# A nearer wait ahead of GpSimd's row fetches in layer 0 and layer 2 of a graph network

## The chip, the cores and the metric

The kernel runs on one core of one Trainium2 chip. The metric is the device time of one execution in microseconds. TensorE is called PE, GpSimd POOL and SyncE SP, as in the profile.

## The reference

Four graph layers run over one graph of 6250 nodes with 128 features and 100000 edges, sorted by destination. Each layer normalises the node features, gathers a row per edge at the edge's source, sums over the edges of each destination, and adds the result to the features. Cut to the sums that the changed code computes:

```python
# layer 0 (graph convolution with edge features)
agg  = segment_sum((nfeat * norm_src)[src], dst)
esum = segment_sum(efeat @ We + be, dst)
# layer 2 (relational, twice): one message table per relation
h    = einsum('ni,rio->rno', x, W)
msg  = h[etype, src]
mean = segment_sum(msg, dst * 8 + etype) / max(count, 1)
x    = mean.sum over relations + x @ W_root + b
```

Layers 1 and 3 are attention layers over the same edges.

## The kernel before, in words

The edges are cut into tiles of 128; there are T = 832 tiles, of which MOST = 829 have rows to fetch, and 52 steps of 16 tiles. Every layer is a pass over the tiles, written out in full (no loop on the chip). In each pass POOL fetches the 128 source rows of a tile from a table in HBM with one indirect DMA into a ring of R slots, VectorE makes a selection matrix from the tile's destinations, PE multiplies the selection by the rows, and VectorE adds the product to an accumulator of the node window that the tile belongs to. Between the tiles of a step PE, ScalarE and VectorE finish one node window: normalise, transpose, project, store.

The three functions of the change are `gather_first` (layer 0, "l0e", ring of R = 16, rows of 512 bytes beside the edge features that SP loads into the other half of each slot, L1028), `gather_relations` (first pass of layer 2, "l2e", R = 16, rows of 1 KB) and `gather_nodes` (second pass of layer 2, "l2f", R = 32, rows of 512 bytes). POOL does nothing in these passes but fetch. Its lines are L999, L2648 and L854. Before every fourth fetch, from tile R on, POOL waits for the semaphore `summed`, which PE raises once per multiplied tile (L1156 and L1157, L2766, L888); in the kernel before the value is `t - R + G`, the last use of the four slots that are written next:

```python
if t >= R and t % G == 0:
    pool.wait_ge(summed, t - R + G)
```

On PE's side, l0e and l2e wait for the rows of each tile by itself; l2f waits at every fourth tile for all four.

What else runs between the tiles of a step: in l0e PE transposes and multiplies the finished sums (L1164, L1165, L1170, L1171), transposes the normalised rows (L1176) and projects them (L1182). In l2e PE multiplies the finished window by the root (L2744) and by the eight relations (L2751, in two halves, at the third and the sixth tile of a step), and SP stores the message block (L2656) and loads the next step's destinations to all partitions (L2661), 512 KB each. In l2f PE transposes (L805) and projects (L818), at the ninth and thirteenth tile.

Of the kernel before, what the change touches and what calls it, by code (L numbers as in the profile page):

```python
# [67 lines left out]
def windows_of(nc, g, engine, first, count=4, at=TA, top=NW - 1):  # L68

    _, values = nc.values_load_multi_w_load_instructions(  # L70
        g.rows[0:1, bass.ds(first + at, count)], engines=(engine,), min_val=0, max_val=top,
        skip_runtime_bounds_check_because="tile_tables clamps every entry to this range")
    return values
# [758 lines left out]
def gather_nodes(nc, g, sem, name, table, index, coef, weights, biases, scale, queries):  # L832

    R = 32
    G = 4
    B = 6
    V = 4
    with Stage(nc, name) as st:
        rows = st.sb("rows", [P, R, D])  # L840
        sel = st.sb("sel", [P, V, G, P])
        ps = [st.ps(f"ps{b}") for b in range(B)]
        nodes = Nodes(nc, g, sem, st, name, weights, biases, False, scale, queries)
        gathered = [sem(f"{name}_g{r}") for r in range(R // G)]
        sel_made, summed, added = sem(name + "_sel"), sem(name + "_summed"), sem(name + "_added")

        with nc.Block() as block:
            @block.gpsimd
            def _(pool):
                for t in range(MOST):  # L850
                    n = t // G
                    if t >= R and t % G == 0:
                        pool.wait_ge(summed, t - R + G)
                    pool.indirect_dma_start(rows[:, t % R, :], None, table, bass.IndirectOffsetOnAxis(index[:, t:t + 1], 0)) \  # L854
                        .then_inc(gathered[n % (R // G)], 16)

            @block.sync
            def _(sp):
                nodes.load(sp)
                for k in range(NW):  # L860
                    if k % nodes.EACH == nodes.EACH - 1:
                        nodes.keep(sp, k)
                    if k >= 1:
                        nodes.store(sp, k - 1)
                nodes.store(sp, NW - 1)
                nodes.land(sp)

            @block.scalar
            def _(act):
                act.wait_ge(nodes.ready, 1)  # L870
                for k in range(NW):
                    act.wait_ge(added, min(S * (k + 3) + 12, T))
                    nodes.stats(act, k)
                    nodes.norm(act, k)
                    nodes.move(act, k)

            @block.tensor
            def _(pe):
                pe.wait_ge(nodes.ready, 1)
                for t in range(T):  # L880
                    n, i, r = t // G, t // S, t % S
                    if t % G == 0:
                        pe.wait_ge(sel_made, n + 1)
                        if t < MOST:
                            pe.wait_ge(gathered[n % (R // G)], 16 * (G * (n // (R // G)) + min(G, MOST - t)))
                    if t % 2 == 0 and t >= B:
                        pe.wait_ge(added, t - B + 2)
                    nc.tensor.matmul(ps[t % B][:, 0:D], sel[:, n % V, t % G, :], rows[:, t % R, :],  # L888
                                     start=True, stop=True).then_inc(summed, 1)
                    if i >= 4 and r == 8:  # L890
                        nodes.turn(pe, i - 4)
                    if i >= 4 and r == 12:
                        nodes.project(pe, i - 4, first=i == 4)
                for k in range(NS - 4, NW):
                    nodes.turn(pe, k)
                    nodes.project(pe, k)

            @block.vector
            def _(dve):
                windows = []  # L900

                def make_sel(n):
                    if n >= V:
                        dve.wait_ge(summed, G * (n - V + 1))
                    for s in range(G):
                        t = n * G + s
                        ins = nc.vector.tensor_scalar(sel[:, n % V, s, :], g.iota[:, :], g.dloc[:, t:t + 1],
                                                      coef[:, t:t + 1], ALU.is_equal, ALU.mult)
                    ins.then_inc(sel_made, 1)

                def add(t):
                    if t % S == 0:
                        windows[:] = windows_of(nc, g, mybir.EngineType.DVE, t, S)
                    x = nodes.x_of(windows[t % S])
                    if t % 2 == 0:
                        dve.wait_ge(summed, t + 2)
                    if t >= 1:
                        dve.wait_ge(added, t)
                    nc.vector.tensor_tensor(x, x, ps[t % B][:, 0:D], ALU.add).then_inc(added, 1)  # L919

                nodes.prepare(dve)
                make_sel(0)
                make_sel(1)
                for n in range(T // G):
                    i, q = n // (S // G), n % (S // G)
                    if n + 2 < T // G:
                        make_sel(n + 2)
                    for s in range(G):
                        add(n * G + s)
                    if q == 1 and i >= 4:  # L930
                        nodes.scales(dve, i - 4)
                    if q == 2 and i >= 4:
                        nodes.join(dve, i - 4)
                    if q == 3 and i >= 4:
                        nodes.add_bias(dve, i - 4, first=i == 4)
                for k in range(NS - 4, NW):
                    nodes.scales(dve, k)
                    nodes.join(dve, k)
                    nodes.add_bias(dve, k)

def gather_first(nc, g, sem, a, queries, own):

    R = 16
    G = 4
    B = 4
    H = 8
# [5 lines left out]
    with Stage(nc, "l0e") as st:  # L954
# [38 lines left out]
        with nc.Block() as block:  # L993
            @block.gpsimd
            def _(pool):
                for t in range(MOST):
                    if t >= R and t % G == 0:
                        pool.wait_ge(summed, t - R + G)
                    pool.indirect_dma_start(rows[:, t % R, 0:D], None, table,  # L999
                                            bass.IndirectOffsetOnAxis(g.src_i[:, t:t + 1], 0)).then_inc(gathered[t % R], 16)  # L1000

# [1604 lines left out]
def gather_relations(nc, g, sem, name, table, index, width, acc, a):  # L2606

    R = 16
    G = 4  # L2610
    B = 5
    LAG = 3
    K3 = 3 * RELS
    with Stage(nc, name) as st:
# [19 lines left out]
        dv, split, selt_made, counted, marked, weighed, coef_made, sel_made, summed, added = (  # L2634
            sem(f"{name}_{k}") for k in ("dv", "split", "selt", "counted", "marked", "weighed", "coef", "sel", "summed",
                                         "added"))
# [5 lines left out]
        with nc.Block() as block:  # L2642
            @block.gpsimd
            def _(pool):
                for t in range(MOST):
                    if t >= R and t % G == 0:
                        pool.wait_ge(summed, t - R + G)
                    pool.indirect_dma_start(rows[:, t % R, :], None, table,  # L2648
                                            bass.IndirectOffsetOnAxis(index[:, t:t + 1], 0)).then_inc(gathered[t % R], 16)

# [234 lines left out]
def layer2(nc, g, sem, a):  # L2885

    with Stage(nc, "l2") as st:
        acc = st.sb("acc", [P, NW * HID])

        gather_relations(nc, g, sem, "l2e", g.msg1_d.rearrange("n (r f) -> (n r) f", r=RELS), g.msg_i, HID, acc, a)

def layer3(nc, g, sem, a, out):

    H = 2
    AW = D + H
    with Stage(nc, "l3") as st:
        acc = st.sb("acc", [P, NW * AW])
        with Stage(nc, "l3t") as tables:  # L2900
            queries = tables.sb("queries", [P, NP])
            gather_nodes(nc, g, sem, "l2f", g.msg2_d.rearrange("n (r f) -> (n r) f", r=RELS), g.msg_i, g.coef,
                         [a["L3_gnn_Wv"], a["L3_gnn_Wk"], a["L3_gnn_Wq"]],
                         [a["L3_gnn_bv"], a["L3_gnn_bk"], a["L3_gnn_bq"]], 64.0 ** -0.5, queries)
            sem.give_back()
            attention_edges(nc, g, sem, "l3te", H, queries, False, acc, AW,
                            lambda st: Outputs(nc, g, sem, st, a, out, acc))
# [92 lines left out]
```

## Time and profile before

| | us |
|---|---|
| median of 3 runs | 6026.54 |
| lowest, highest run | 6025.05, 6029.79 |
| span of the profiled execution | 7205.4 |
| POOL busy in it | 4079.2 (57%) |
| PE busy in it | 4349.8 (60%) |
| VectorE busy in it | 3857.3 (54%) |

The profiled execution is known by its span alone; no other time of it is given. It is longer than every timed run by about 1179 us. Busy times count an engine's instructions without its waits. A PE time is modelled at its end. "Issue" is time in which an engine waited for nothing that the profile shows. A fetch's time on POOL is that of its issue; its landing is not among the rows. A wait that is put down to a DMA of another stage, or to "remote", is one whose releaser the profile could not tell.

### The profile page before, as it was taken

What the parts mean: (1) busy time and instruction counts of PE and PEld (TensorE: products, weight loads), DVE (VectorE), ACT (ScalarE), POOL (GpSimd) and SP (SyncE); (2) the same over time, 40 slices, a digit from 0 to 9 for tenths busy, and PEclk for the clock granted to TensorE, in tenths of its full rate; (3) what the DMA queues carried; (4) which work ended last, traced back from release to release, by engine and by line L of the source; (5) the groups of instructions that cost most, each with busy time, mean ns of one, the idle gap of its engine ahead of it and who ended that gap; (6) DMA issues with size and microseconds to landing.
All of it is one profiled execution on the core that took longest, in us unless ns stands there. A gap on an engine that the chain in (4) does not pass through costs nothing. (4 is left out here: it accounts for less than half of the span.)

```text
span 7205.4 us, 86034 instructions
## 1 busy us (share of the span) xinstructions
PE 4349.8 (60%) x19030; PEld 3531.2 (49%) x19030; DVE 3857.3 (54%) x11927; ACT 1461.9 (20%) x3928; POOL 4079.2 (57%) x4191
## 2 busy tenths in 40 slices
PE   4777778746566656795666666344343456665656
PEld 4666666635555555444444444233333345555555
DVE  7444444446566656745555555344444455666655
ACT  4122222212222222350111111000000112222222
POOL 1666666646566554106666665666666555555553
PEclk9977776766666666897888888555555566667676
DMA  2433333323333334274444444122222333333333
GB/s 49 126 108 102 100 101 100 100 87 109 106 108 107 105 99 84 82 286 125 135 129 136 128 136 109 51 60 56 59 56 59 74 100 113 106 110 113 108 112 64
DMA packets 426775, 738.44 MB, mean 102 GB/s; under 512 B 100523, under 2 KB 280580, under 8 KB 419701
## 3 DMA queue, kind: packets, MB, share of 16 engines
q0 software_dynamic: 173200, 436.47, 23.0%
q1 hardware_dynamic: 244484, 289.62, 12.2%
q10 hardware_dynamic: 8592, 6.82, 0.3%
q8 instruction: 176, 2.88, 0.2%
q14 instruction: 323, 2.64, 0.1%
HBM read 613.55 MB, written 120.20 MB: 102 GB/s over the span
## 5 line engine op out<-in xcount | busy, mean ns | idle before, releaser
L1637 POOL DMA_INDIRECT xh<-pair_d,src_i x1658 | 1647.5, 994 | 1191.6 <-issue 459.2
L2648 POOL DMA_INDIRECT l2e_rows<-msg_d,msg_i x829 | 804.8, 971 | 749.3 <-POOLq L61 315.4
L999 POOL DMA_INDIRECT l0e_rows<-node_d,src_i x829 | 789.0, 952 | 450.4 <-issue 220.4
L854 POOL DMA_INDIRECT l2f_rows<-msg_d,msg_i x829 | 782.7, 944 | 431.4 <-issue 231.9
L1156 PE MATMUL l0e_ps<-l0e_rows,l0e_sel 128*128 128x256 f32 x1664 | 795.2, 575 | 282.3 <-issue 232.8
L888 PE MATMUL l2f_ps<-l2f_rows,l2f_sel 128*128 128x128 f32 x1664 | 413.1, 417 | 600.1 <-DVE xh L919 501.0
L2766 PE MATMUL l2e_ps<-l2e_rows,l2e_sel 128*128 128x256 f32 x1664 | 490.0, 427 | 422.5 <-DVE l2e_sel L2860 396.4
L888 PEld LDWEIGHTS l2f_ps<-l2f_rows,l2f_sel 128*128 128x128 f32 x1664 | 367.3, 310 | 674.7 <-issue 394.9
L2825 DVE TENSOR_TENSOR l_acc<-l_acc,l2e_ps 128x256 f32 x832 | 349.4, 420 | 498.4 <-DMA node_d<-l1t_queries 329.0
L919 DVE TENSOR_TENSOR xh<-xh,l2f_ps 128x128 f32 x832 | 238.3, 286 | 675.5 <-DMA tb_raw<-edges_d,starti 470.7
L1221 DVE TENSOR_TENSOR early_acc<-early_acc,l0e_ps 128x264 f32 x832 | 356.8, 429 | 441.0 <-PE l0e_ps L1157 168.6
L2766 PEld LDWEIGHTS l2e_ps<-l2e_rows,l2e_sel 128*128 128x128 f32 x1664 | 328.6, 212 | 534.6 <-DVE l2e_sel L2860 424.8
L1681 PE MATMUL l1te_pq<-l1t_queries,l1te_wide 128*128 x1664 | 353.9, 380 | 327.8 <-DVE l1te_prod L1895 225.6
L1681 PE MATMUL l3te_pq<-l3t_queries,l3te_wide 128*128 x1664 | 350.1, 377 | 314.2 <-DVE l3te_prod L1895 216.2
L1156 PEld LDWEIGHTS l0e_ps<-l0e_rows,l0e_sel 128*128 128x128 f32 x1664 | 367.9, 271 | 326.9 <-issue 252.1
L1157 PEld LDWEIGHTS l0e_ps<-l0e_of_rel,l0e_sel 128*128 128x128 f32 x1664 | 452.2, 272 | 103.0
L2022 DVE TENSOR_TENSOR l1acc_acc<-l1acc_acc,l1te_ps 128x144 f32 x832 | 246.6, 296 | 466.9 <-DMA l0e_rows<-in_edge_attr_dram 259.9
L1681 PEld LDWEIGHTS l1te_pq<-l1t_queries,l1te_wide 128*128 128x128 f32 x1664 | 310.9, 279 | 372.6 <-issue 372.3
L2022 DVE TENSOR_TENSOR l_acc<-l_acc,l3te_ps 128x130 f32 x832 | 234.9, 282 | 475.7 <-remote 263.7
L1681 PEld LDWEIGHTS l3te_pq<-l3t_queries,l3te_wide 128*128 128x128 f32 x1664 | 306.7, 276 | 353.8 <-issue 352.5
L1733 PE MATMUL l1te_ps<-l1te_ve,l1te_sel 128*128 128x144 f32 x1664 | 398.4, 402 | 19.9 <-DVE l1te_ve L2006 18.2
L1733 PE MATMUL l3te_ps<-l3te_ve,l3te_sel 128*128 128x130 f32 x1664 | 361.0, 378 | 54.8 <-DVE l3te_ve L2006 18.1
(454 smaller groups left out, 8180.8 us busy)
## 6 DMA issues: line engine op xcount, KB each, us to landing
l0e_rows<-in_edge_attr_dram SPq DMA_DIRECT2D x832, 64.0 KB
msg_d<-l1t_queries SPq DMA_DIRECT2D x50, 1024.0 KB, 3.9
l1te_local<-local_d SPq DMA_DIRECT2D x52, 512.0 KB
l2e_local<-local_d SPq DMA_DIRECT2D x52, 512.0 KB
l3te_local<-local_d SPq DMA_DIRECT2D x52, 512.0 KB
xh<-pair_d,src_i POOLq DMA_INDIRECT x1658
msg_d<-l2e_msg SPq DMA_DIRECT2D x50, 512.0 KB
l0e_rows<-node_d,src_i POOLq DMA_INDIRECT x829
```

The source lines that it names most:

```text
L854: pool.indirect_dma_start(rows[:, t % R, :], None, table, bass.IndirectOffsetOnAxis(index[:, t:t + 1], 0)) \
L888: nc.tensor.matmul(ps[t % B][:, 0:D], sel[:, n % V, t % G, :], rows[:, t % R, :], start=True, stop=True).then_inc(summed, 1)
L999: pool.indirect_dma_start(rows[:, t % R, 0:D], None, table, bass.IndirectOffsetOnAxis(g.src_i[:, t:t + 1], 0)).then_inc(gathered[t % R], 16)
L1156: nc.tensor.matmul(ps[r % B][:, 0:2 * D], sel[:, r // G % 2, r % G, :], rows[:, r, :], start=True, stop=True)
L1157: nc.tensor.matmul(ps[r % B][:, 2 * D:W0], sel[:, r // G % 2, r % G, :], of_rel[:, r // G % 2, r % G, :], start=True, stop=True).then_inc( ...
L1221: nc.vector.tensor_tensor(one, one, ps[s][:, 0:W0], ALU.add).then_inc(added, 1)
L1637: pool.indirect_dma_start(rows[:, t % R, :], None, g.pair_d, bass.IndirectOffsetOnAxis(g.src_i[:, t:t + 1], 0)).then_inc(gathered[n % RG], 16)
L1681: mm = nc.tensor.matmul(pq[n % 2][:, i * D:(i + 1) * D], wide[:, n // GS % 2, n % GS * G + i, :], queries[:, bass.ds(ws[i] * D, D)], start ...
L1733: nc.tensor.matmul(slot(t), sel[:, n % V, t % G, :], ve[:, n % V, t % G, :], start=True, stop=True).then_inc(summed, 1)
L2022: nc.vector.tensor_tensor(part, part, slot(t), ALU.add).then_inc(added, 1)
L2648: pool.indirect_dma_start(rows[:, t % R, :], None, table, bass.IndirectOffsetOnAxis(index[:, t:t + 1], 0)).then_inc(gathered[t % R], 16)
L2766: nc.tensor.matmul(ps[t % B][:, 0:width], sel[:, t // G % 2, t % G, :], rows[:, t % R, :], start=True, stop=True).then_inc(summed, 1)
```

## The change

In the three functions a constant NEAR = 8 takes the place of R in the wait's condition and in its value. The slots, the order of the fetches and everything on the other engines stay. So ahead of the fetches of tiles t to t + 3 POOL waits until t - 4 tiles are multiplied, in place of t - 12 (l0e, l2e) or t - 28 (l2f).

```diff
@@ gather_nodes
     R = 32
+    NEAR = 8
...
-                    if t >= R and t % G == 0:
-                        pool.wait_ge(summed, t - R + G)
+                    if t >= NEAR and t % G == 0:
+                        pool.wait_ge(summed, t - NEAR + G)
@@ gather_first
     R = 16
+    NEAR = 8
...
-                    if t >= R and t % G == 0:
-                        pool.wait_ge(summed, t - R + G)
+                    if t >= NEAR and t % G == 0:
+                        pool.wait_ge(summed, t - NEAR + G)
@@ gather_relations
     R = 16
+    NEAR = 8
...
-                    if t >= R and t % G == 0:
-                        pool.wait_ge(summed, t - R + G)
+                    if t >= NEAR and t % G == 0:
+                        pool.wait_ge(summed, t - NEAR + G)
```

## Rows read from the trace of the kernel before

**Rows 1.** Head of the page.
```profile
span 7205.4 us, 86034 instructions
```

**Rows 2.** Stretches l0e, l2e, l2f: us, busy PE, PEld, DVE, ACT, POOL (instructions); clock, DMA.
```profile
207.00:1454.00 1247.00, 973.05 (x3760) 824.38 (x3760) 601.17 (x2037) 286.00 (x782) 788.98 (x829) 0.75 0.38 104
3235.00:4489.00 1254.00, 786.47 (x3516) 570.72 (x3517) 691.26 (x1974) 135.79 (x346) 804.79 (x829) 0.84 0.44 130
4507.00:5712.00 1205.00, 476.03 (x1808) 387.98 (x1808) 499.48 (x1903) 104.40 (x389) 782.70 (x829) 0.57 0.23 56
```

**Rows 3.** The page's groups, fetches: xcount | busy, mean ns | idle before, releaser.
```profile
L1637 POOL DMA_INDIRECT xh<-pair_d,src_i x1658 | 1647.5, 994 | 1191.6 <-issue 459.2
L2648 POOL DMA_INDIRECT l2e_rows<-msg_d,msg_i x829 | 804.8, 971 | 749.3 <-POOLq L61 315.4
L999 POOL DMA_INDIRECT l0e_rows<-node_d,src_i x829 | 789.0, 952 | 450.4 <-issue 220.4
L854 POOL DMA_INDIRECT l2f_rows<-msg_d,msg_i x829 | 782.7, 944 | 431.4 <-issue 231.9
```

**Rows 4.** l2f: a step in time order, a stretch's busy time; waits (total, times, longest).
```profile
5101.37 0.47 PE L805 MATMUL l2f_pt<-ident,l2f_pairs 128*128 128x128 f32 x1 [2.68 <-issue]
...
5103.35 1.49 PE L818 MATMUL l2f_po<-l2f_w,l2f_ht 128*128 128x384 f32 x2
...
5109.60:5116.40 6.80, 0.00 (x0) 0.00 (x0) 0.00 (x0) 0.00 (x0) 2.94 (x4) 0.52 0.15 39
...
5116.65 0.94 POOL L854 DMA_INDIRECT l2f_rows<-msg_d,msg_i  x1 [3.20 <-DMA tb_raw<-edges_d,starti]
...
5119.78 1.79 PE L888 MATMUL l2f_ps<-l2f_rows,l2f_sel 128*128 128x128 f32 x6 [1.19 <-DVE xh L919]
...
DVE xh L919 <- DMA tb_raw<-edges_d,starti: 470.7, 84, 10.5
```

**Rows 5.** Start of l2f in order of time: start, length, engine, line [idle before, releaser].
```profile
4511.34 0.95 POOL L854 DMA_INDIRECT l2f_rows<-msg_d,msg_i  x1 [0.30 <-issue]
...
4514.26 2.05 PE L888 MATMUL l2f_ps<-l2f_rows,l2f_sel 128*128 128x128 f32 x8 [11.91 <-DMA l2f_rows<-msg_d,msg_i]
...
4516.33 0.95 POOL L854 DMA_INDIRECT l2f_rows<-msg_d,msg_i  x1 [0.30 <-issue]
...
4517.59 0.94 POOL L854 DMA_INDIRECT l2f_rows<-msg_d,msg_i  x1 [0.30 <-issue]
...
4518.97 1.40 PE L888 MATMUL l2f_ps<-l2f_rows,l2f_sel 128*128 128x128 f32 x5 [2.66 <-DMA l2f_rows<-msg_d,msg_i]
```

**Rows 6.** Busy time by stretch, the six outside the five gathering passes: their sum.
```profile
sum 739.00, PE 492.95 PEld 306.39 DVE 440.53 ACT 302.54 POOL 55.84; mean PE 82.16 PEld 51.07 DVE 73.42 ACT 50.42 POOL 9.31
```

**Rows 7.** One step of l2e: in order of time, and busy time of one stretch.
```profile
3901.92 1.88 PE L2751 MATMUL l2e_pm<-l2e_w,l2e_ht 128*128 128x512 f32 x4
...
3904.77 1.32 POOL L2648 DMA_INDIRECT l2e_rows<-msg_d,msg_i  x1 [0.30 <-PE l2e_ps L2766]
...
3907.60 0.34 SPq L2656 DMA_DIRECT2D msg_d<-l2e_msg  x1
...
3908.00 0.42 SPq L2661 DMA_DIRECT2D l2e_local<-local_d  x1
...
3907.60:3912.60 5.00, 3.30 (x26) 2.27 (x24) 1.77 (x6) 0.34 (x2) 3.78 (x4) 1.00 0.71 246
```

**Rows 8.** One step of l0e: busy time of the step, and PE's other work in order.
```profile
899.70:923.60 23.90, 17.64 (x73) 15.15 (x72) 11.38 (x40) 5.97 (x18) 15.31 (x17) 0.71 0.36 101
...
902.57 0.77 PE L1170 MATMUL l0e_pz<-l0e_w,l0e_z 128*128 128x128 f32 x2
...
903.14 0.63 PE L1171 MATMUL l0e_pz<-l0e_w,l0e_z 128*128 128x128 f32 x2
...
903.56 0.42 PE L1176 MATMUL l0e_ph<-ident,l0e_hc 128*128 128x128 f32 x1
...
909.06 1.63 PE L1182 MATMUL l0e_pv<-l0e_w,l0e_ht 128*128 128x384 f32 x2
```

## The prediction

> **What bounds the kernel now.** I read the span first [rows 1], then the three passes that the diff touches, as stretches [rows 2]: 1247, 1254 and 1205 us, in which no engine is full. TensorE (PE) is busy for 78%, 63% and 40% of them, GpSimd (POOL) for 63 to 65%. In the profiled execution GpSimd is therefore not the bound of these passes: the fetch lines of the page [rows 3] show it idle for 450 us in layer 0 and 431 us in the second pass of layer 2 ahead of its fetches, of which 220 and 232 us are the fixed gap between two fetches ("issue") and the rest mostly waits on the products; in the first pass of layer 2 it is 749 us, 315 of them ahead of the pass. That is the ring at work: the fetches run as far ahead as it lets them.
>
> The profiled execution is not the execution that is timed. Its span is 7205.4 us [rows 1], 1179 us more than the median of 6026.5 us, and the reader should see where such time can sit. In the second pass of layer 2 ("l2f") there is a stretch of 6.8 us in which PE, VectorE and ScalarE do nothing, and GpSimd issues four fetches and stops [rows 4]; VectorE's waits of this kind in l2f are 84, 470.7 us in all, for 52 steps of 16 tiles. Whether the timed runs have the holes no row shows. What the rows do show is a floor: a fetch takes 0.952, 0.971, 0.944 and 0.994 us in layer 0, the first and the second pass of layer 2, and the attention passes [rows 3], and each follows the one before at 0.30 us [rows 5]. So 829 x 1.252 + 829 x 1.271 + 829 x 1.244 + 1658 x 1.294 = 1038 + 1054 + 1031 + 2145 = 5268 us of GpSimd in the five gathering passes. What lies outside them takes 739 us [rows 6]. Together 6007 us, 0.3% under the median. My estimate is that in the timed runs the holes are mostly gone and GpSimd's cadence is close to being the bound of all five passes, which makes any microsecond that GpSimd waits a microsecond of the result.
>
> **What the change does.** It removes and adds no work: no fetch, no product, no DMA. The wait rides on the first of four fetches; ten more of some 600 such fetches get one (two more in each ring of 16, six in the ring of 32), at no cost of their own. It moves the moment: the fetch of tiles t to t+3 needs all products through tile t-5. GpSimd can be four to eight tiles ahead of PE, and no longer up to 16 or 32. Behind the waiting fetch on GpSimd stand only later fetches; who waits for them is PE, and behind PE VectorE's additions. SP's transfers wait on other counts and are not held.
>
> **The loop that is new, and its slack.** From the end of the issue of tile t-5 to GpSimd's turn for tile t pass four fetches and five gaps, 4 x 0.95 + 5 x 0.30 = 5.3 us. In that time tile t-5 must land and be multiplied, or GpSimd stops. For the landing I take the start of l2f, where PE waits for nothing but the fetched rows [rows 5]: the fourth fetch ends at 4512.29 and PE starts at 4514.26, the eighth ends at 4517.28 and PE starts at 4518.97. So landing and signal take at most 1.7 us. This bound serves for all three passes.
>
> l2f: PE takes four tiles at once. The same rows give the slack directly: the first four products end at 4516.31, and GpSimd's turn for the ninth tile is at 4517.59: 1.28 us to spare, with GpSimd never stopped. What eats it, once a step, is PE's other work between the tiles: the projection, 1.49 us, and a transpose, 0.47 us, in neighbouring groups [rows 4]. The projection alone overruns by 1.49 - 1.28 = 0.21 us, both together by 0.68. From 11 to 35 us over 52 steps; nothing in the rows says how much they add up, so I take the middle, 24 us.
>
> First pass of layer 2 ("l2e"): PE's busy time is 786.5 / 832 = 0.95 us a tile, other work included [rows 2]. A tile is asked for 4 x 0.971 + 5 x 0.30 = 5.38 us after its issue, so the slack is 5.38 - 1.7 - 0.95 = 2.7 us. PE's message products between two tiles, 1.88 us, fit [rows 7]. What may not fit is SP's pair of transfers of 512 KB each (sizes from the code), issued 0.4 us apart; the stretch behind them moves 246 GB/s at 71% of the DMA engines' time [rows 7]. 1 MB at that rate is 4.3 us, so a fetch that shares the engines with it lands between 0 and 4.3 us later. Over the slack that is 0 to 1.6 us a step, 0 to 83 us; I take half, 42 us, since the engines are neither free nor full there. Today this is hidden by the rows already fetched.
>
> Layer 0 ("l0e"): a step of 16 tiles has 17.64 us of PE [rows 8], 1.1 us a tile; slack 5.3 - 1.7 - 1.1 = 2.5 us. PE's other work comes in pieces of 0.77 + 0.63 + 0.42 = 1.82 us and 1.63 us [rows 8]. Each fits; if PE has not caught up between them, they overrun by 3.45 - 2.5 = 0.95 us, 49 us in all. PE's 17.64 us against 16 x 1.252 = 20.0 us of GpSimd say that it mostly does catch up, so I take a third, 16 us.
>
> Once per pass GpSimd also stops after eight fetches while the stage is set up; that is a fetch or two, and I leave it in the range. Sum: 24 + 42 + 16 = **82 us**. Against the profiled execution that would be 7205 + 82; against the median, 6026.5 + 82 = **6108 us**, 1.4% slower. All bounds low give 11 us more, all high 35 + 83 + 49 = 167.
>
> **Rivals.** First, GpSimd is the bound and the wait never ends last: then fetched rows do not pile up at all, and the place of the wait is of no matter. This is the start of l2f prolonged over all passes [rows 5]. It holds as long as PE's delay behind a landing stays under 1.28 us in l2f, 2.7 in l2e and 2.5 in l0e, and the first that passes these decides against it. Time: **6026 us**. For it speaks the floor of 6007; against it the 1.49 us projection and SP's 1 MB.
>
> Second, the holes are in the timed runs too. Then PE works in bursts behind each, and the fetched pile feeds the burst. In l2f GpSimd's own wait ends at 5116.65, at the end of the hole [rows 4]; the fourth fetch from there ends 3 x 1.244 + 0.94 = 4.67 us later, and lands by 5123.0. PE wants that group at the third tile of its six records, at 5119.78 + 2/3 x 1.79 = 5121.0. Late by 2.0 us, 104 us over 52 steps; with l2e and l0e at their upper bounds, 104 + 83 + 49 = 236 us: **6262 us**. For it speaks every step of the profile; against it that the median is 1179 us shorter than that profile.
>
> Third, a small gain: fetches now issue at other moments beside VectorE. One fetch of l2e took 1.32 us where 0.94 is usual [rows 7]. If one such a step moves out of its way, 0.38 x 52 = 20 us: **6006 us**. But nothing says that the new moments are quieter.
>
> **The numbers.** Forecast 6108 with 0.48; second rival 0.23; first 0.20; third 0.09. A measurement of this kernel tells about 0.2%, 12 us, from no change. Slower is the forecast and the second rival, 0.71; same the first, 0.20; faster the third, 0.09. The range runs from 6010, which takes in the first rival and half of the third, to 6270, above all three upper bounds (6194) and the second rival. The slower cases' own range is 6037 to 6270.
>
> **What would show it.** In the changed kernel's profile the waits of the fetches on the products must grow in all three passes, and PE must now wait for fetched rows, which it hardly did. My steps are right if PE's new waits stand in l2e behind SP's two transfers, in l2f at the third and fourth group of a step, and little in l0e. If the waits of GpSimd grow and PE waits for no rows, the first rival is right. I am wrong if a pass becomes shorter, or if l0e loses most.

## The result, and the profile after

The changed kernel takes 6128.2 us (median of 4 runs) against 6027.3 us before: 101 us more, ratio 1.0166, 95% interval 1.0155 to 1.0178. Forecast were 6108 us in a range of 6010 to 6270.

The span in [rows 1], 7205.4 us, belongs to one recorded execution of the kernel before that was unlike the timed ones. A second recorded execution of the same kernel has a span of 6028.7 us, within 0.1% of the timed runs. It is the one to compare with, and it stands here as "before, second profile". Head of the page, the three passes as stretches (length, busy PE, PEld, DVE, ACT, POOL, clock, DMA share, GB/s), and the fetches of the page's groups (busy, mean ns of one, idle before):

```profile
span 6028.7 us, 86034 instructions
...
185.00:1232.00 1047.00, 845.49 (x3760) 728.88 (x3760) 604.89 (x2043) 288.05 (x782) 787.28 (x829) 0.82 0.45 124
2720.00:3791.00 1071.00, 842.32 (x3516) 578.48 (x3517) 698.42 (x1974) 136.16 (x346) 800.15 (x829) 0.85 0.51 153
3810.00:4862.00 1052.00, 478.82 (x1808) 397.23 (x1808) 506.13 (x1904) 104.75 (x390) 783.53 (x829) 0.53 0.25 64
...
L2648 POOL DMA_INDIRECT l2e_rows<-msg_d,msg_i x829 | 800.1, 965 | 568.1 <-POOLq L61 315.9
L854 POOL DMA_INDIRECT l2f_rows<-msg_d,msg_i x829 | 783.9, 946 | 289.1 <-issue 243.2
L999 POOL DMA_INDIRECT l0e_rows<-node_d,src_i x829 | 787.3, 950 | 260.5 <-issue 225.0
```

The same views of the changed kernel; they answer to [rows 1 to 3]:

```profile
span 6127.2 us, 86034 instructions
...
185.00:1255.00 1070.00, 883.71 (x3760) 763.34 (x3760) 604.64 (x2043) 288.17 (x782) 789.21 (x829) 0.77 0.44 121
2747.00:3890.00 1143.00, 888.93 (x3515) 605.38 (x3516) 695.77 (x1974) 136.17 (x346) 799.46 (x829) 0.82 0.48 143
3909.00:4962.00 1053.00, 481.94 (x1808) 399.88 (x1808) 505.85 (x1902) 104.71 (x390) 784.94 (x829) 0.53 0.26 64
...
L2651 POOL DMA_INDIRECT l2e_rows<-msg_d,msg_i x829 | 799.5, 964 | 648.6 <-POOLq L61 316.3
L855 POOL DMA_INDIRECT l2f_rows<-msg_d,msg_i x829 | 785.2, 947 | 288.9 <-issue 239.3
L1001 POOL DMA_INDIRECT l0e_rows<-node_d,src_i x829 | 789.2, 952 | 281.8 <-issue 220.5
```

Two things are to be seen. In the second profile of the kernel before, l0e and l2f take 1047 and 1052 us for 829 fetches at 1.25 us, 1036 us: GpSimd's cadence is the bound, as the prediction estimated and [rows 2] did not show. Taken between the two, l0e grew by 23 us, l2e by 72 and l2f by 1. GpSimd's idle time ahead of its fetches grew by 21, 80 and 0 us: what it waits in mid-pass, the kernel loses. At the end of a pass it is otherwise: there GpSimd is done first, and from its last fetch to PE's last product of l2e pass 18.0 us in the kernel before and 10.7 in the changed one, so that some 7 us of the 80 cost nothing.

A step of l2e in the changed kernel, in order of time (start, length, engine, line; idle before and its releaser), shows how:

```profile
3304.16 0.34 SPq L2659 DMA_DIRECT2D msg_d<-l2e_msg  x1
...
3304.56 0.42 SPq L2664 DMA_DIRECT2D l2e_local<-local_d  x1
...
3306.04 0.66 PE L2769 MATMUL l2e_ps<-l2e_rows,l2e_sel 128*128 128x256 f32 x2
...
3310.44 0.95 POOL L2651 DMA_INDIRECT l2e_rows<-msg_d,msg_i  x1 [0.30 <-issue]
3310.56 2.22 PE L2769 MATMUL l2e_ps<-l2e_rows,l2e_sel 128*128 128x256 f32 x4 [3.86 <-DMA l2e_rows<-msg_d,msg_i]
...
3313.05 0.94 POOL L2651 DMA_INDIRECT l2e_rows<-msg_d,msg_i  x1 [1.66 <-PE l2e_ps L2769]
...
3319.23 1.07 POOL L2651 DMA_INDIRECT l2e_rows<-msg_d,msg_i  x1 [1.49 <-PE l2e_ps L2769]
...
3303.30:3306.70 3.40, 3.02 (x18) 1.83 (x16) 1.86 (x7) 1.35 (x4) 2.48 (x4) 1.00 0.70 234
3310.50:3316.00 5.50, 5.32 (x22) 4.12 (x23) 3.15 (x8) 0.00 (x0) 3.23 (x4) 0.50 0.29 86
```

SP issues its two transfers of 512 KB. PE multiplies the tiles whose rows are there, the last at 3306.04, and then stands for 3.86 us with the next rows not landed. GpSimd has issued four fetches meanwhile and now waits for the products: the fetch at 3313.05 starts 1.66 us behind the end of the last one, 1.36 us more than the fixed gap. Four tiles later it waits again, 1.49 us. The last two rows are stretches before and behind PE's stand: the granted clock was 1.00 before it and 0.50, the lower of its two levels, behind it, and a tile's product takes 1.11 us (3310.56, two tiles) in place of 0.66 (3306.04).

### The profile page after: what moved, and what is told of

Its sections match the earlier page's. It is cut to its first block and busy times, and to the rows that moved or that the text cites. A ratio compares the mean times of both kernels' runs of the same rounds, so it can differ in the third digit from the quotient of the medians.

```text
span 6127.2 us, 86034 instructions
## 1 busy us (share of the span) xinstructions
PE 4242.9 (69%) x19030; PEld 3403.7 (56%) x19030; DVE 3876.5 (63%) x11927; ACT 1463.9 (24%) x3928; POOL 4059.0 (66%) x4191
## 5 line engine op out<-in xcount | busy, mean ns | idle before, releaser
L1639 POOL DMA_INDIRECT xh<-pair_d,src_i x1658 | 1621.4, 978 | 569.6 <-issue 485.9
L1158 PE MATMUL l0e_ps<-l0e_rows,l0e_sel 128*128 128x256 f32 x1664 | 721.7, 527 | 204.6 <-DVE early_acc L1223 83.5
L2769 PE MATMUL l2e_ps<-l2e_rows,l2e_sel 128*128 128x256 f32 x1664 | 571.5, 471 | 218.8 <-DMA l2e_rows<-msg_d,msg_i 186.7
L1683 PE MATMUL l1te_pq<-l1t_queries,l1te_wide 128*128 x1664 | 333.5, 364 | 274.3 <-DVE l1te_prod L1897 260.1
L1158 PEld LDWEIGHTS l0e_ps<-l0e_rows,l0e_sel 128*128 128x128 f32 x1664 | 334.7, 247 | 238.4 <-issue 180.0
L1683 PEld LDWEIGHTS l1te_pq<-l1t_queries,l1te_wide 128*128 128x128 f32 x1664 | 288.3, 261 | 320.2 <-issue 319.8
L1159 PEld LDWEIGHTS l0e_ps<-l0e_of_rel,l0e_sel 128*128 128x128 f32 x1664 | 414.7, 249 | 86.8
L1683 PEld LDWEIGHTS l3te_pq<-l3t_queries,l3te_wide 128*128 128x128 f32 x1664 | 286.2, 259 | 301.3 <-issue 300.0
L1735 PE MATMUL l1te_ps<-l1te_ve,l1te_sel 128*128 128x144 f32 x1664 | 367.3, 378 | 13.0 <-DVE l1te_ve L2008 12.7
L1735 PEld LDWEIGHTS l1te_ps<-l1te_ve,l1te_sel 128*128 128x128 f32 x1664 | 322.5, 267 | 21.4 <-DVE l1te_ve L2008 15.8
```

The costliest lines, as they stand in the source:

```text
L1158: nc.tensor.matmul(ps[r % B][:, 0:2 * D], sel[:, r // G % 2, r % G, :], rows[:, r, :], start=True, stop=True)
L1159: nc.tensor.matmul(ps[r % B][:, 2 * D:W0], sel[:, r // G % 2, r % G, :], of_rel[:, r // G % 2, r % G, :], start=True, stop=True).then_inc( ...
L1639: pool.indirect_dma_start(rows[:, t % R, :], None, g.pair_d, bass.IndirectOffsetOnAxis(g.src_i[:, t:t + 1], 0)).then_inc(gathered[n % RG], 16)
L1683: mm = nc.tensor.matmul(pq[n % 2][:, i * D:(i + 1) * D], wide[:, n // GS % 2, n % GS * G + i, :], queries[:, bass.ds(ws[i] * D, D)], start ...
L1735: nc.tensor.matmul(slot(t), sel[:, n % V, t % G, :], ve[:, n % V, t % G, :], start=True, stop=True).then_inc(summed, 1)
L2769: nc.tensor.matmul(ps[t % B][:, 0:width], sel[:, t // G % 2, t % G, :], rows[:, t % R, :], start=True, stop=True).then_inc(summed, 1)
```

## The experiments

**The kernel before, once more.** No edit.

> The kernel before, unchanged, for a second profile. Theory (GpSimd's cadence bounds the timed runs, the holes belonged to that one recorded execution): a span near 6026 us without the holes, the fetches of l0e, l2e and l2f at 1.25 us from one to the next, and GpSimd's waits on products below 60 us in the three passes together (they were 556 us in the profile shown). Rival (the holes are in the timed runs): again stretches of 6 to 7 us in every step of l2f with all engines still.

Measured: span 6028.7 us, rows above. The waits of GpSimd on products come to 27.6, 22.5 and 9.1 us in l0e, l2e and l2f, and none is longer than 0.5 us, so they are the fixed gap under another name. VectorE's waits at L919 in l2f, 470.7 us of an unknown releaser in [rows 4], are now these:

```profile
DVE xh L919 <- PE l2f_ps L888: 410.4, 187, 5.3
```

Released by products, none longer than 5.3 us; holes of 6.8 us are not among them. The longest stretch of l2f in which PE, VectorE and ScalarE all stand is 9.2 us in the first profile and 3.0 us in the second. (GpSimd's waits on products in the first profile come to 614 us by the rows of the same view, and not to the 556 of the expectation.) The second rival had its ground in the holes, and falls. That recording by itself makes holes is not shown either: this execution was recorded too, with the same 86034 instructions. What made the first one slow stays open.

**Each pass alone.** The three lines of the diff, in one function each.

```diff
@@ gather_relations (near_l2e); gather_first (near_l0e); gather_nodes (near_l2f)
+    NEAR = 8
...
-                    if t >= R and t % G == 0:
-                        pool.wait_ge(summed, t - R + G)
+                    if t >= NEAR and t % G == 0:
+                        pool.wait_ge(summed, t - NEAR + G)
```

> The near wait in the first pass of layer 2 alone. Theory (SP's two transfers make the rows of tiles 10 to 13 of a step land 1 to 3 us late, and GpSimd now waits for the product of tile 11): +60 to +85 us of the 101, near 6100 us. Rival (the three passes lose alike): +34 us, 6061 us.

> The near wait in layer 0 alone. Theory: +10 to +25 us, nearly all of it once, at the start of the pass, where GpSimd stops after eight fetches while the stage is set up. Rival (PE's other work between the tiles overruns the slack in each step): +34 to +49 us, spread over the pass.

> The near wait in the second pass of layer 2 alone. Theory: 0 to +10 us, since the projection that was to overrun the slack stands at a group whose next fetch has time. Rival (the predicted 24 us): the projection of each step stops GpSimd by about 0.5 us.

Measured against 6025.6 us: l2e 6099.9 (+74.4 us, ratio 1.0122, interval 1.0107 to 1.0138); l0e 6045.1 (+19.5, 1.0030, 1.0018 to 1.0043); l2f 6025.4 (-0.2, 0.9999, 0.9990 to 1.0008). Together 93.7 of the 101 us; what is missing lies within the intervals, so nothing larger than these three losses is needed. GpSimd's waits on products in the run of each function, by total, times and longest:

```profile
POOL l2e_rows L2649 <- PE l2e_ps L2767: 135.3, 169, 5.8
```
```profile
POOL l0e_rows L1000 <- PE l0e_ps L1158: 52.8, 106, 6.3
```
```profile
POOL l2f_rows L855 <- PE l2f_ps L889: 18.7, 38, 3.0
```

Less 0.30 us for each, which is the gap that a fetch has anyway, they are 85, 21 and 7 us. The first two are about the loss. The 7 us of l2f cost nothing: they stand in the last 16 tiles of the pass,

```profile
POOL l2f_rows L855 <- PE l2f_ps L889: 8.5, 5, 3.0
```

and there PE ends the pass, not GpSimd. From the last fetch to the last product pass 15.4 us in the kernel before and 8.7 us here.

**SP's two transfers set apart.** In the changed kernel the store takes its place behind the next load in SP's order; all work is kept.

```diff
@@ gather_relations
-                    if s >= LAG + 3:
-                        store(s - LAG - 3)
-                for k in range(NS - LAG - 3, NW):
+                    if s >= LAG + 4:
+                        store(s - LAG - 4)
+                for k in range(NS - LAG - 4, NW):
```

> The changed kernel, but in the first pass of layer 2 SP's store of a message block waits behind the next load of destinations in SP's order, so that the load (512 KB) starts early in a step and the store (512 KB) at its middle, not both at the middle. Theory (the pair of transfers is what makes rows land late): no fetch is delayed by more than about 2 us, GpSimd's waits in l2e fall from 100 to 20 to 50 us, and 50 to 75 us of the 101 come back, near 6065 us. Rival (PE's own work between the tiles is what delays the product of tile 11): no more than 15 us come back.

Measured: 6069.2 us against 6028.7 (ratio 1.0066, 1.0052 to 1.0080): +40 us in place of +101, so 60 us came back. The rows of a step, and GpSimd's waits in the pass:

```profile
3304.50 0.32 SPq L2664 DMA_DIRECT2D l2e_local<-local_d  x1
...
3313.21 0.34 SPq L2659 DMA_DIRECT2D msg_d<-l2e_msg  x1
...
3318.16 0.95 POOL L2651 DMA_INDIRECT l2e_rows<-msg_d,msg_i  x1 [0.30 <-issue]
3318.38 1.47 PE L2769 MATMUL l2e_ps<-l2e_rows,l2e_sel 128*128 128x256 f32 x4 [2.65 <-DMA l2e_rows<-msg_d,msg_i]
...
3326.30 1.08 POOL L2651 DMA_INDIRECT l2e_rows<-msg_d,msg_i  x1 [0.95 <-PE l2e_ps L2769]
...
POOL l2e_rows L2651 <- PE l2e_ps L2769: 47.3, 80, 5.6
```

The transfers are now 8.7 us apart. In this step PE still stands for its rows, 2.65 us, the longest such time of the pass, but that is inside the slack: GpSimd issues on at its fixed gap, and waits only at 3326.30, 0.65 us above the gap. The waits fall from 129 us (161 times) in the changed kernel to 47 us (80 times); less the gap, from 81 to 23 us. In the 47 steps between tiles 64 and 812 the fetch that needs the product of tile 11 of its step waits more than 0.4 us above the gap 42 times in the changed kernel, and never here. Of the 23 us that are left, 5 are at the ninth fetch of the pass and 8.5 at its last three groups. The same order in the kernel before:

> The kernel before with the order of SP's two transfers in the first pass of layer 2 as in the earlier run that set them apart, as a version that might beat both. Theory (with the ring of 16 a late landing is covered, and GpSimd's cadence bounds the pass): within 10 us of the kernel before. Rival (the pair also delays something in the kernel before): 15 to 20 us faster, the waits of GpSimd that the pass has left.

Measured: 6038.9 us against 6037.4 (1.0003, 0.9994 to 1.0012), no difference. With the ring's full lead the late rows cost nothing, and no version here beats the kernel before.

**Four tiles more of lead, in l2e alone.** NEAR = 12 in `gather_relations`, 8 in the other two.

> The changed kernel with a wait for products up to 12 tiles behind their end in the first pass of layer 2, 8 in the two others. Theory (5 us more of slack cover a landing that is 2.6 us late): nearly all of that pass's 74 us come back, 6050 to 6060 us. Rival (any bound short of the full ring costs in proportion): half of them, near 6090 us.

Measured: 6046.4 us against 6028.7 (1.0030, 1.0020 to 1.0041): +18 us, which is what layer 0 costs by itself. The 74 us of l2e are gone, and the pass is back at its length before:

```profile
2745.00:3816.00 1071.00, 838.72 (x3515) 575.12 (x3516) 696.32 (x1973) 135.60 (x346) 800.04 (x829) 0.85 0.51 153
```

So the cost is not in proportion to the lead: it is the part of one delay that overhangs the slack.

**Where layer 0 loses.** The near wait in l0e from tile 64 on, only up to tile 64, and from tile 256 on.

```diff
@@ gather_first
+    NEAR = 8
...
+                    back = NEAR if t >= 64 else R    # l0e_late
+                    back = NEAR if t < 64 else R     # l0e_start
+                    back = NEAR if t >= 256 else R   # l0e_later
-                    if t >= R and t % G == 0:
-                        pool.wait_ge(summed, t - R + G)
+                    if t >= back and t % G == 0:
+                        pool.wait_ge(summed, t - back + G)
```

> Layer 0 alone with the near wait, but only from tile 64 on; the first 64 tiles keep the wait of the kernel before. Theory (the 20 us of layer 0 are lost once, at the start of the pass): 0 to +6 us against the kernel before. Rival (they are lost a little in every step): +15 to +20 us.

> Layer 0 alone, the near wait only up to tile 64, then the wait of the kernel before. Theory (layer 0 loses its 20 us at the start, while the stage's set-up keeps VectorE from the additions, and PE, at about GpSimd's pace, leaves no later slack to win them back): +13 to +20 us. Rival (a little in every step): 0 to +4 us.

> Layer 0 alone, the near wait only from tile 256 on, when the backlog of the start is gone. Theory: 0 to +6 us, of GpSimd's waits in 36 steps. Rival (a little in every step): +10 to +16 us.

Measured: from tile 64, +10.8 us (1.0014, 1.0005 to 1.0023), more than the theory allowed and less than the rival; up to tile 64, +15.4 us (1.0027, 1.0017 to 1.0036); from tile 256, -1.4 us (0.9999, 0.9990 to 1.0008). The loss is at the start. The waits of GpSimd of more than the gap ahead of tiles 0 to 31, with the near wait up to tile 64, and with them two rows of PE and one of a store that ScalarE's queue sends:

```profile
196.80 1.19 PE L1158 MATMUL l0e_ps<-l0e_rows,l0e_sel 128*128 128x256 f32 x2 [29.71 <-DMA l0e_rows<-in_edge_attr_dram]
...
202.33 0.94 POOL L1001 DMA_INDIRECT l0e_rows<-node_d,src_i  x1 [6.34 <-PE l0e_ps L1159]
...
213.25 0.94 POOL L1001 DMA_INDIRECT l0e_rows<-node_d,src_i  x1 [0.94 <-PE l0e_ps L1159]
...
218.49 1.02 ACTq L540 DMA_DIRECT2D ends_d<-early_ends  x2
...
219.16 0.94 POOL L1001 DMA_INDIRECT l0e_rows<-node_d,src_i  x1 [1.09 <-PE l0e_ps L1159]
...
226.82 0.94 POOL L1001 DMA_INDIRECT l0e_rows<-node_d,src_i  x1 [2.97 <-PE l0e_ps L1159]
...
231.84 1.19 PE L1158 MATMUL l0e_ps<-l0e_rows,l0e_sel 128*128 128x256 f32 x2 [5.29 <-DMA l0e_rows<-node_d,src_i]
...
237.37 0.94 POOL L1001 DMA_INDIRECT l0e_rows<-node_d,src_i  x1 [5.86 <-PE l0e_ps L1159]
```

17.2 us in five waits, 15.7 without the gaps, about what was lost. The two long ones stand behind a time in which PE waits for a DMA. At 196.80 it is the edge features that SP loads: PE starts so late that GpSimd, eight tiles on, has to stop. At 231.84 it is the fetched rows of tile 20: by the trace that fetch, issued at 219.16, landed 11.5 us behind its end, where 1.6 us is usual, and those of tiles 21 to 27 took 4.4 to 10.5 us. They were issued behind ScalarE's store of 218.49; that this store holds them up is the likely reading, and no run took it away. Ahead of the three short waits PE stands for no more than 0.5 to 1.7 us at a time, while VectorE's set-up comes between the additions. Why the run from tile 64 still lost 10 us its profile shows, in the first fetch that has the near wait, and in a stretch ahead of it:

```profile
258.00:275.00 17.00, 17.00 (x54) 14.57 (x54) 7.26 (x21) 1.96 (x3) 6.38 (x8) 0.50 0.48 144
...
274.67 0.94 POOL L1001 DMA_INDIRECT l0e_rows<-node_d,src_i  x1 [8.79 <-PE l0e_ps L1159]
```

PE is still behind there in that execution, and this one fetch pays for it. PE is busy all the time, at a granted clock of 0.50, and its tiles follow each other at 1.28 us, no faster than GpSimd's 1.25, so it does not catch up. The start is not over by tile 64.

**The loop in the open.** NEAR = 4 in all three functions: every fetch of four waits for all products before it.

```diff
-    NEAR = 8
+    NEAR = 4
```

> All three passes with a wait for the products of every tile before the four that are fetched (4 tiles behind their end): the slack of the near wait less four fetches, 5.0 us. It puts the loop from issue to product in the open. With a landing of 1.2 to 1.7 us and one to four products behind it, each group of four would take 6.7 to 9 us in place of 5.0: 207 groups, three passes, 1050 to 2500 us more than the kernel before. If the loop is shorter than I think (landing hidden by other fetches), less than 1000 us.

Measured, one run: 8509.6 us, 2481 us more, at the upper end of what was expected. Over 3 x 207 groups that is 4.0 us a group on top of 5.0. The three passes and GpSimd's waits:

```profile
184.00:1987.00 1803.00, 1136.88 (x3760) 960.65 (x3760) 609.89 (x2044) 290.73 (x784) 783.28 (x829) 0.60 0.25 72
3477.00:5444.00 1967.00, 1167.27 (x3518) 720.01 (x3519) 722.33 (x1975) 136.15 (x346) 792.48 (x829) 0.69 0.28 83
5462.00:7343.00 1881.00, 496.64 (x1808) 412.68 (x1808) 509.33 (x1903) 104.73 (x390) 789.22 (x829) 0.52 0.13 36
...
POOL l2e_rows L2651 <- PE l2e_ps L2769: 975.6, 207, 10.9
POOL l2f_rows L855 <- PE l2f_ps L889: 895.2, 207, 7.3
POOL l0e_rows L1001 <- PE l0e_ps L1159: 821.6, 207, 11.9
```

All 207 groups wait, 4.0 to 4.7 us each on average, by pass. That is the loop from the end of a fetch's issue to its product, with nothing to hide it; the near wait of 8 leaves four fetches, 5.0 us, more for it. The prediction put this loop at 1.7 + 0.95 us in l2e and 1.7 + 1.1 us in l0e; here it is 4.7 and 4.0 us, so its slack of 2.7 and 2.5 us was too wide, at least at the clock of this run. The granted clock in these stretches fell, to 0.60 and 0.69 of full speed in l0e and l2e from 0.82 and 0.85, so some of the 4 us is a slower PE; how much was not separated.

## Why the prediction was right, point by point

**The bound.** Right, and the point on which all else rests. The sum of GpSimd's cadence and the stretches outside, 6007 us, was 0.3% under the median, and the second profile has the passes at that cadence: the five take 5257 us from first to last fetch, forecast 5268, and the rest takes 772 us, forecast 739. It could not be read from [rows 2], where GpSimd was 63 to 65% busy; it came from setting the fetch's price against the timed median, not against the profiled span.

**The loop and its slack.** Right in kind. That a wait on GpSimd is lost for good, and that only delays over the slack cost anything, is what near_l2e (85 us of waits above the gap, 74 us lost), l2e_12 (nothing lost with 5 us more) and sp_apart (PE stands for up to 2.65 us, and hardly a fetch waits) show. Waits at the end of a pass are the exception, as in l2f. The landing of at most 1.7 us is about right where no other transfer is in the way (the trace's medians are 1.5 to 1.8 us, for the tiles whose landing it has) and wrong beside one.

**l2e, 42 us forecast, 74 measured.** The cause was the one named, SP's two transfers: with them apart 60 us return. By the trace the rows of tile 11 of a step land 4.5 us (median) behind the end of their issue, those of tiles 6 and 7 1.8 us, so 2.7 us late of the at most 4.3. That this was "hidden by the rows already fetched" is wrong: PE stands for late rows in the kernel before too (second profile, first line: total, times, longest), if less than in the changed one (second line). What the ring hid it from is GpSimd, which issued on while PE caught up.

```profile
PE l2e_ps L2766 <- DMA l2e_rows<-msg_d,msg_i: 139.6, 86, 4.1
PE l2e_ps L2769 <- DMA l2e_rows<-msg_d,msg_i: 186.7, 92, 4.8
```

The term was mis-sized at "0 to 1.6 us a step", which has one wait a step where there are two. Summed by tile over the trace of the changed kernel, GpSimd's waits above the gap are 47 us at the fetch that needs tile 11, near the 42 forecast; 19 us at the next one that waits, four tiles on; 5 us at the ninth fetch of the pass, and 9 us at its last three groups, most of which cost nothing. The second wait goes with PE's clock: in the 47 steps between tiles 64 and 812 it is over 0.4 us above the gap 17 times, and each time the mean granted clock of the 6 us before it is 0.60 or less.

**l0e, 16 us forecast, 19.5 measured, for another reason.** The step that failed is PE's other work that overruns 2.5 us of slack in each step: from tile 256 on the near wait costs -1.4 us, and by its interval no more than 5. The 20 us are the item that the prediction left aside as "a fetch or two, and I leave it in the range", the stop after eight fetches while the stage is set up. It is not once but five waits of up to 6.3 us: PE starts late for want of the edge features, rows land up to 11.5 us behind their issue in the middle of the set-up, and at half clock PE does not win back what it has lost. That the sum of 16 is near 19.5 is luck.

**l2f, 24 us forecast, none measured.** The step that failed is the slack of 1.28 us, read at the start of the pass [rows 5], where PE started 1.97 us behind the end of the fourth fetch. (The middle of 11 and 35 us is also 23 and not 24.) Rows of the second profile of the kernel before give the slack in the middle of the pass, and the projection in it:

```profile
4201.06 2.04 PE L888 MATMUL l2f_ps<-l2f_rows,l2f_sel 128*128 128x128 f32 x8 [2.83 <-DVE l2f_sel L907]
...
4204.81 0.95 POOL L854 DMA_INDIRECT l2f_rows<-msg_d,msg_i  x1 [0.30 <-issue]
...
4211.65 1.49 PE L818 MATMUL l2f_po<-l2f_w,l2f_ht 128*128 128x384 f32 x2
...
4212.93 1.49 PE L888 MATMUL l2f_ps<-l2f_rows,l2f_sel 128*128 128x128 f32 x6
...
4214.80 0.94 POOL L854 DMA_INDIRECT l2f_rows<-msg_d,msg_i  x1 [0.30 <-PE l2f_ps L888]
```

A plain group starts 1.58 us behind its fourth fetch and ends at 4203.10, and GpSimd's next group is due at 4204.81: 1.71 us. The group with the projection ends at 4214.42, with 0.38 us left. The projection fits, barely, and costs nothing; what waits the run of l2f alone has are at the end of the pass.

The sum, 82 against 94 by pass and 101 in all, was nearer than its terms, and that is in part luck: one too high, one too low, one right by another cause.

**The rivals.** The first (the wait never ends last) is true of l2f but for the end of the pass; elsewhere it was decided, as said, by SP's 1 MB, and by the start of l0e. Its premise, that fetched rows do not pile up, holds: PE waits for rows in the kernel before. The second (holes, 6262 us) falls with the second profile. By the Trainium skill's "NOTIFIC — the notification-queue block", section 7.1 on overflow, recording may hold an engine back; the second recorded execution has no such holes, so the rule may be at work in the first but does not make them each time. The third (a small gain) did not show in any run. Of the signs named, GpSimd's waits grew in all three passes and those of l2e stand behind SP's transfers; those of l2f stand at the end of the pass and not in each step, and PE's waits for rows were not new.

## What to carry to other kernels

Where an engine that issues fetches is the bound, its lead over the consumer must cover the longest single delay of a landing or a product, and not the mean one. Below that the loss is the overhang, once per delay, and more where the consumer's clock falls while it stands; above it further slots bring nothing (in l2e a lead of 8 tiles lost 74 us, 12 lost none). Here transfers that another queue sends in a pair set that longest delay, so look at them, and at the set-up at a stage's start, before a ring is made shorter. When the profiled span is far from the timed median, multiply out the busiest issuer's cadence and set it against the median before trusting a busy share.

## What was not expected of the hardware

One recorded execution took 7205.4 us where a second one of the same kernel took 6028.7 us, with PE, VectorE and ScalarE still together for up to 9.2 us in l2f, where the second has 3.0 at most; its cause is open. The row fetch has the same price of about 0.95 us and a gap of 0.30 us whether its rows are 512 bytes (0.946 us, l2f) or 1 KB (0.965 us, l2e), and the gap is there in both recorded executions. Behind a pair of 512 KB transfers on SP's queue, 0.4 us apart, the row fetches of tile 11 of a step landed 4.5 us behind their issue and not 1.8, and at the start of l0e, behind ScalarE's store, up to 11.5 us.
